# A decoder layer on one core: cross-attention with block-diagonal keys, and its stages as a pipeline over batches

## The chip, the cores and the metric

The kernel runs on one core of a Trainium2 chip. The metric is the time of one execution on the device, in microseconds (us); less is better. The engines named here are TensorE (PE, with its weight loads as PEld), VectorE (DVE), ScalarE (ACT), GpSimd (POOL) and SyncE (SP), which only issues transfers.

## The reference

For 4 batches of 512 tokens of width 256 (16 heads of 16), and a context of 64 rows a batch:

```
x = layernorm(x + attn(x) @ wo.T)
q2 = x @ wq + bq;  k2 = ctx @ wk + bk;  v2 = ctx @ wv + bv        # 16 heads, 64 keys
x = layernorm(x + softmax(q2 k2^T / 4) v2 @ xwo + bo)
probs = softmax(x @ router_w.T);  two largest of 8 experts a token
x = layernorm(x + sum_e w_e * gelu(x @ w1[e].T) @ w2[e].T)
```

Everything is float32. The two choices of expert make the logits' precision matter, so the kernel keeps scores at about float32's precision even where it uses narrower operands.

## The kernel before, in words

Each engine has its own list of instructions, in the order in which the program writes them; semaphores tie the lists together. There is no planner: the order is written out by hand.

**Self-attention** runs in 16 units (batch x four heads), `unit(u)`. A unit has 16 score tiles (128 keys x 512 queries), an exponential for each on ScalarE (L807), and four groups of `pv` (L1397), which multiply the values in and carry a column of ones for the sum. Row maxima run two units ahead, so the last two units (14 and 15) have none; they carry `context_v` and `context_k` instead, the projections of the context. The result, transposed, lies in `oT`.

**Ends.** `end_of_attention(ph, b, others)` finishes a batch; `ph` is 0 behind self-attention, 1 behind cross-attention. Each of its 4 tiles of 128 tokens passes through `turn_o` (L1455, four transposes), a reciprocal and a product on VectorE (L1055, L1057), `turn_back` (L1465, two transposes), a copy on ScalarE (L828), `out_proj` (L1473), and `add_residual` on VectorE (L1065, L1067, L1069). Once four tiles have their variance GpSimd raises it to the power -1/2 (L680), and VectorE writes the normalised rows (L1079). Each of these steps has two PSUM banks in turn. `turn_x` (L1485) transposes the rows again, ScalarE copies them (L832).

**Cross-attention, operands.** `q2_proj` (L1505) gives q2 transposed. q2 and k2 are cut into three bfloat16 parts (ScalarE L847 and L851, VectorE L1101, GpSimd L685), stored to DRAM and loaded back as a *stack*: 96 rows for each head, the six products of parts that matter one above another. A score is then one bfloat16 matmul of 96 rows. SyncE does these stores and loads (L498 to L514) and puts the maxima, also in three parts, into three more rows by small transfers (L391).

**Cross-attention, work.** `max2_tile` (L1523) makes the scores of 128 queries for 16 heads, 16 matmuls of 64 columns, and VectorE reduces 1024 columns (L1114). `max2_turn` and `max2_T` turn the maxima. `exp2_tile` (L1539) makes one head's scores, 64 keys x 512 queries with its maximum subtracted, and ScalarE takes the exponential (L882): 16 a batch, on 64 partitions. `pv2` (L1546) does four heads at once; VectorE copies the result to `oT` (L1139). The maxima of batch b+2 are made within batch b.

**Order around the change.** The ends of self-attention of all four batches come first, with turn and projection of the batch before them in between; then the cross-attention of four batches; then the ends of cross-attention with the routing of the batch two before them. Routing is about 21 small steps on VectorE (L1189 to L1228), two small groups on TensorE (`logits` L1615, `positions` L1624), and 8 indirect transfers a batch on GpSimd (L728). When all 32 have landed and the plan of tiles is made (L1260 on), tile metadata is loaded, rows are gathered, and 39 tiles go through their experts (L1658, L1669). Expert weights `wexp` are loaded by SyncE, one expert a cross-attention batch and five behind it (L520).

## Time and profile before

| what | value |
|---|---|
| median of 3 runs | 835.06 us (833.75 to 840.89) |
| the profiled execution | 832.12 us, its span 829.9 us |
| TensorE busy | 690.3 us, 83% of the span |
| VectorE busy | 353.1 us, 43% |
| ScalarE busy | 284.1 us, 34% |
| GpSimd busy | 219.3 us, 26% |
| mean granted TensorE clock | 0.909 of full |

Busy time is from the first to the last cycle of an instruction. Matmuls are pipelined: four in a row that are printed as one line last as long as four pitches and one latency. The idle time in brackets behind a row is that just before it on its engine, with what ended it. Self-attention ends at 269.2 us with the copy of its last unit, cross-attention's last unit at 423 us, the last rows before routing are normalised at 476.4 us, the first expert matmul is at 518.3 us, and the last at 806 us.

### The profile page before, as it was taken

The numbers are of one execution on the slowest core, as the hardware profiler recorded it, in microseconds if no ns is written. First come the engines' busy times: TensorE is split into PE (matmuls) and PEld (weight loads), VectorE is DVE, ScalarE is ACT, GpSimd is POOL, SyncE is SP. The second block draws the span as 40 slices with busy tenths as digits, with TensorE's granted clock in tenths as the row PEclk, the third lists the DMA queues.
The fourth block names the chain that finished last, engine by engine and source line by source line (L and its number), as shares of the span: only waits on it lengthen the run. The fifth ranks groups of instructions, "written<-read, shape, count | busy, mean of one in ns | idle before, by whom it ended". The sixth has DMA issues, their size and how long they took to land.

```text
span 829.9 us, 11914 instructions
## 1 busy us (share of the span) xinstructions
PE 690.3 (83%) x4099; PEld 444.7 (54%) x4100; DVE 353.1 (43%) x766; ACT 284.1 (34%) x513; POOL 219.3 (26%) x275
## 2 busy tenths in 40 slices
PE   6899999999998865757778520999999999999970
PEld 3322233322222644422147420899999999999960
DVE  3687877788972666643358750000000000000004
ACT  2246656667775233324632110111111111111112
POOL 2211111110120223210201672233333333333322
PEclk9869999999999989677899855999999999999995
DMA  5974133325343268592337233466666656666506
GB/s 158 190 166 82 15 80 75 78 70 105 58 138 89 21 104 124 95 139 55 99 111 249 52 54 111 137 177 180 181 184 178 176 159 178 178 179 183 169 11 203
DMA packets 69544, 103.60 MB, mean 125 GB/s; under 512 B 15556, under 2 KB 54909, under 8 KB 67966
## 3 DMA queue, kind: packets, MB, share of 16 engines
q1 hardware_dynamic: 56766, 90.44, 43.3%
q0 software_dynamic: 8512, 8.44, 6.2%
q10 hardware_dynamic: 4224, 4.19, 1.8%
q8 instruction: 22, 0.36, 0.2%
q14 instruction: 20, 0.16, 0.1%
HBM read 82.95 MB, written 21.40 MB: 126 GB/s over the span
## 4 chain that ended last, share of the span: by engine, by line
PE 69%; DVE 11%; DMA 7%; ACT 3%; POOL 3%; issue 3%; SPq 2%; DVEq 0%; POOLq 0%; ACTq 0%
PE ps L1658 17%; PE ps L1669 16%; PE ps L1397 7%; PE ps L1388 7%; PE ps L1322 6%; DVE nmx L966 3%; POOL metas L728 3%; PE ps L1473 3%; PE ps L1340 2%; PE ps L1546 2%; PE ps L1539 2%; ACT probs L807 2%; PE ps L1505 2%; DVE xr L1079 2%; DMA qst<-scr_q 1%
## 5 line engine op out<-in xcount | busy, mean ns | idle before, releaser
L807 ACT ACTIVATE probs<-ps 128x512 f32<-128x512 f32 x256 | 135.5, 603 | 92.0 <-PE ps L1388 91.3
L966 DVE TENSOR_REDUCE nmx<-ps 128x1 f32<-128x512 f32 x256 | 159.7, 679 | 15.7 <-PE ps L1322 15.2
L1658 PEld LDWEIGHTS ps<-xtT,w1c 128*128 128x128 f32 x1248 | 147.3, 194 | 4.3 <-issue 2.4
L1658 PE MATMUL ps<-xtT,w1c 128*128 128x128 f32 x1248 | 147.7, 277 | 1.8 <-ACT xtT L919 1.8
L1284 DVE TENSOR_SCALAR yw<-ps,mt 128x256 f32<-128x256 f32 x39 | 18.9, 484 | 292.0 <-PE ps L1669 292.0
L1669 PE MATMUL ps<-wexp,hidT 128*128 x624 | 141.0, 379 | 0.0
L1669 PEld LDWEIGHTS ps<-wexp,hidT 128*128 128x128 f32 x624 | 115.6, 190 | 14.1
L925 ACT ACTIVATE hidT<-ps 128x1024 f32<-128x1024 f32 x39 | 39.9, 1024 | 230.0 <-PE ps L1658 230.0
L767 POOL DMA_INDIRECT acc<-yw,mt x39 | 61.7, 1583 | 172.0 <-DVE yw L1284 172.0
L1322 PE MATMUL ps<-kst,qst 96*128 96x512 bf16 x256 | 99.2, 409 | 4.6 <-DVE nmx L966 3.3
L1388 PE MATMUL ps<-qst,kst 99*128 99x512 bf16 x256 | 93.4, 390 | 1.6 <-ACT probs L807 1.2
L1397 PE MATMUL ps<-probs,vu 128*32 128x512 f32 x512 | 68.2, 605 | 1.9 <-ACT probs L807 1.4
L1388 PEld LDWEIGHTS ps<-qst,kst 99*128 99x128 bf16 x256 | 23.6, 98 | 84.5 <-ACT probs L807 57.1
L882 ACT ACTIVATE probs<-ps 64x512 f32<-64x512 f32 x64 | 35.4, 587 | 41.5 <-PE ps L1539 41.4
L1322 PEld LDWEIGHTS ps<-kst,qst 96*128 96x128 bf16 x256 | 25.4, 99 | 44.4 <-DVE nmx L966 23.9
L759 POOL DMA_INDIRECT xt<-x2d,mt x39 | 40.8, 1046 | 31.5 <-DMA mt<-metas 12.0
L1539 PE MATMUL ps<-qst,k2st 99*64 99x512 bf16 x64 | 27.0, 468 | 13.9 <-DMA qst<-mT 8.5
L1647 PE MATMUL ps<-identf,xt 128*128 128x128 f32 x78 | 15.2, 277 | 27.9 <-DMA xt<-x2d,mt 27.9
L728 POOL DMA_INDIRECT metas<-meta,slot x32 | 31.6, 988 | 22.4 <-DVE slot L1226 13.9
L596 POOL TENSOR_TENSOR m<-nmx,one 128x16 bf16<-128x16 f32 x16 | 3.5, 217 | 126.5 <-DVE nmx L966 126.5
L1485 PE MATMUL ps<-identf,xr 128*128 128x128 f32 x64 | 13.7, 353 | 22.4 <-DVE xr L1079 21.6
L680 POOL TENSOR_TENSOR rstd<-ve,halves 128x4 f32<-128x4 f32 x8 | 10.9, 1364 | 72.0 <-DVE ve L1072 71.9
(177 smaller groups left out, 673.9 us busy)
## 6 DMA issues: line engine op xcount, KB each, us to landing
w1c<-in_w1T SPq DMA_DIRECT2D x39, 1024.0 KB, 5.4
wexp<-in_w2T SPq DMA_DIRECT2D x8, 1024.0 KB, 5.6
kst<-scrk SPq DMA_DIRECT2D x48, 128.0 KB, 7.0
qst<-scr_q SPq DMA_DIRECT2D x24, 256.0 KB, 9.1
qst<-scrq SPq DMA_DIRECT2D x8, 384.0 KB, 4.7
scr_q<-parts SPq DMA_DIRECT2D x4, 768.0 KB, 4.3
xTb<-in_xT SPq DMA_DIRECT2D x4, 512.0 KB, 8.4
qst<-scrq SPq DMA_DIRECT2D x8, 256.0 KB, 5.4
```

The source lines that it names most:

```text
L728: pool.indirect_dma_start(metas, bass.IndirectOffsetOnAxis(slot[b % 2][:, k * QT + t:k * QT + t + 1], 0), meta[k][:, 2 * (QT * b + t):2 * ...
L759: pool.indirect_dma_start(xt[t % 2][:, :], None, x2d, bass.IndirectOffsetOnAxis(slot_meta(t, 0).bitcast(U32), 0), **checked()).then_inc(s_ ...
L767: pool.indirect_dma_start(acc, bass.IndirectOffsetOnAxis(slot_meta(t, 0).bitcast(U32), 0), yw[t % 2][:, :], None, **checked(), compute_op= ...
L807: act.activation(probs[n % 8][:, :], ps[:, 4 + n % 3, :], ACT.Exp).then_inc(s_exp, 1)
L925: act.activation(hidT[j % 2][:, :], bank(2 * (j % 2), 2), ACT.Gelu).then_inc(s_h, 1)
L966: dve.tensor_reduce(nmx[w % 2][:, k:k + 1], ps[:, ring_bank("max", w, k), :], AX.X, ALU.max, negate=True).then_inc(s_mfree, 1)
L1322: pe.matmul(ps[:, ring_bank("max", w, k), :], qst[0:ROWS, q_cols(w, h) + qt * P:q_cols(w, h) + (qt + 1) * P], kst[0:ROWS, k_cols(w, h):k_c ...
L1388: pe.matmul(ps[:, 4 + n % 3, :], kst[:, k_cols(u, h) + kt * P:k_cols(u, h) + (kt + 1) * P], qst[:, q_cols(u, h):q_cols(u, h) + S], start=T ...
L1397: mm = pe.matmul(ps[VW * h:VW * (h + 1), 7, :], vu[u % 2][:, (kt * HG + h) * VW:(kt * HG + h + 1) * VW], probs[(kt % 2) * HG + h][:, :], s ...
L1539: pe.matmul(ps[0:SC, 4 + h % 2, :], k2st[0:MROWS, ds((h * NB + b) * SC, SC)], qst[0:MROWS, ds((b * H + h) * S, S)], start=True, stop=True) ...
L1658: mm = pe.matmul(ps[:, 2 * (j % 2) + f // 4, f % 4 * P:(f % 4 + 1) * P], w1c[j % 2][:, k * FF + f * P:k * FF + (f + 1) * P], xtT[j % 2][:, ...
L1669: mm = pe.matmul(ps[:, 4 + j % 2, 0:D], hidT[j % 2][:, f * P:(f + 1) * P], wexp[:, ds(e * EW + f * D, D)], start=(f == 0), stop=(f == KF - 1))
```

## The change

- **Keys in diagonal blocks.** `k2h[m]` and `k2l[m]` hold, for the 8 heads of half m and each batch, 64 columns per head in which only that head's 16 rows of k2 are not zero. They are made on chip from k2 and the mask `mine`: 128 x 2048 elements each, two by VectorE (`k2_high_blocks`), two by GpSimd (`k2_blocks`). k2 and q2 are each cut in two: a high part, which is the value cast to `float32r`, and a low part, value minus high part, `float32r` too. No part goes to DRAM; the stacks, their stores and loads, and GpSimd's `split_q2` are gone.
- **Scores.** `max2_tile(b, i)` is one bank of 512 columns (8 heads x 64 keys, 128 queries): three `float32r` matmuls of 512 columns, high x high, high x low, low x high; 8 a batch. `exp2_tile(b, p)` does two heads on 128 partitions: three such matmuls, and one bfloat16 matmul of `pick` with the turned maxima, which subtracts them; 8 a batch. Exponentials are 8 a batch on 128 partitions. `pv2` multiplies pairs of heads with the block-diagonal `v2bd`, two products a group. The copy of the result moves from VectorE to ScalarE. `context_v` is done twice, for partitions 0 to 63 and 64 to 127.
- **Order.** The end of batch 0's self-attention is put between the score tiles of unit 15. Then come seven stages. Stage n holds the end of self-attention of batch n (e1), cross-attention of batch n-1 (x), the end of cross-attention of batch n-2 (e2) and routing of batch n-3 (r), interleaved on each engine by hand. The ends have one bank for each step now; maxima, scores and q2 share banks 5 and 6 (`ring2`).
- **Transfers.** SyncE issues the stores of the normalised rows (ScalarE did). Experts 0, 1 and 7 are loaded once self-attention is done, 2 and 3 after the last cross-attention, then 4 and 5, and 6 after the last logits. GpSimd issues a batch's 8 scatters in one piece, behind the power of the stage before.

The diff, cut to its core:

```diff
+    def tiles_of(ph, b):
+        return QT * E_AT[ph, b]
+    def ring2(i):
+        return 6 - i % 2
...
-        def split_q2(b):
-            pool.wait_ge(s_q2c[2], b + 1)
...
+        def k2_blocks(out, part, m):        # GpSimd
+            pool.tensor_tensor(out[:, :].rearrange("p (b h k) -> p b h k", h=HB, k=SC),
+                               part[:, m * NB * SC:(m + 1) * NB * SC].rearrange("p (b k) -> p b k", k=SC).unsqueeze(2)
+                               .to_broadcast([P, NB, HB, SC]),
+                               mine[:, :].unsqueeze(1).unsqueeze(3).to_broadcast([P, NB, HB, SC]), ALU.mult).then_inc(s_k2l, 1)
+        for m in range(KD):
+            k2_blocks(k2l[m], k2tl, m)
...
+        for n in range(NB + 3):             # GpSimd
+            if n < NB:
+                rstd_of(0, n)
+                add_bias(n)
+            if 0 <= n - 2 < NB:
+                rstd_of(1, n - 2)
+            if n == NB + 2:
+                pool.wait_ge(s_on, NE_TILES)
+                for i in range(2):
+                    pool.memset(xt[i][:, :], 0.0).then_inc(s_xt0, 1)
+            if n >= 3:
+                scatter_metas(n - 3)
...
+            dve.tensor_copy(k2th[:, :], k2t[:, :]).then_inc(s_k2p, 1)
+            dve.tensor_tensor(k2tl[:, :], k2t[:, :], k2th[:, :], ALU.subtract).then_inc(s_k2p, 1)
...
+        def first_end():                    # VectorE, in unit 15
+            norm_o(0, 0, 0)
+            norm_o(0, 0, 1)
+            k2_high_blocks(0)
+            for t in range(2):
+                norm_o(0, 0, 2 + t)
+                add_residual(0, 0, t)
+            k2_high_blocks(1)
+            for t in range(2, QT):
+                add_residual(0, 0, t)
...
+        FIRST_END = {5: 0, 7: 1, 9: 2, 11: 3, 13: 4, 15: 5}   # TensorE, by score tile of unit 15
...
+        def max2_tile(b, i):
+            t, m = i // KD, i % KD
+            pe.wait_ge(s_ql, b + 1)
+            if i >= 2:
+                pe.wait_ge(s_m2f, NP * b + i - 1)
+            at, keys = m * S + t * P, slice(b * HB * SC, (b + 1) * HB * SC)
+            high, low = qh[b % 2][:, at:at + P], ql[b % 2][:, at:at + P]
+            pe.matmul(ps[:, ring2(i), :], high, k2h[m][:, keys], start=True, stop=False)
+            pe.matmul(ps[:, ring2(i), :], high, k2l[m][:, keys], start=False, stop=False)
+            pe.matmul(ps[:, ring2(i), :], low, k2h[m][:, keys], start=False, stop=True).then_inc(s_m2r, 1)
...
+        def exp2_tile(b, p):
+            pe.wait_ge(s_m2c, b + 1)
+            if p >= 2:
+                pe.wait_ge(s_exp2, NP * b + p - 1)
+            pe.matmul(ps[:, ring2(p), :], k2h[m][:, at:at + P], high, start=True, stop=False)
+            pe.matmul(ps[:, ring2(p), :], k2h[m][:, at:at + P], low, start=False, stop=False)
+            pe.matmul(ps[:, ring2(p), :], k2l[m][:, at:at + P], high, start=False, stop=False)
+            pe.matmul(ps[:, ring2(p), :], pick[:, p * P:(p + 1) * P], mT2[:, :], start=False, stop=True).then_inc(s_e2, 1)
...
+        def stage(n):                       # TensorE; "if" lines left out
+            turn_x(1, r, 0); turn_x(1, r, 1)
+            e1_step(0);  max2_tile(x, 0); max2_tile(x, 1)
+            e1_step(1);  max2_tile(x, 2); max2_tile(x, 3);  logits(r, range(QT))
+            e1_step(2);  max2_tile(x, 4); max2_tile(x, 5)
+            e1_step(3);  max2_tile(x, 6); max2_tile(x, 7)
+            e1_step(4);  e1_step(5);  e2_step(0);  max2_turn(x)
+            e2_step(1);  exp2_tile(x, 0); exp2_tile(x, 1)
+            e2_step(2);  exp2_tile(x, 2); exp2_tile(x, 3);  turn_x(0, e1, 0); turn_x(0, e1, 1);  pv2(x, 0)
+            e2_step(3);  positions(r);  exp2_tile(x, 4); exp2_tile(x, 5);  pv2(x, 1)
+            e2_step(4);  exp2_tile(x, 6); exp2_tile(x, 7);  pv2(x, 2);  q2_proj(e1, 0)
+            e2_step(5);  q2_proj(e1, 1);  pv2(x, 3)
...
+        def stage(n):                       # VectorE; "if" lines left out
+            norm_o(0, e1, 0);  row_max2(x, 0); row_max2(x, 1)
+            norm_o(0, e1, 1);  row_max2(x, 2); row_max2(x, 3)
+            norm_o(0, e1, 2);  add_residual(0, e1, 0);  row_max2(x, 4); row_max2(x, 5);  router_logits(r)
+            norm_o(0, e1, 3);  add_residual(0, e1, 1);  row_max2(x, 6); row_max2(x, 7);  max2_parts(x);  probabilities(r)
+            add_residual(0, e1, 2); add_residual(0, e1, 3);  norm_o(1, e2, 0);  max2_T(x)
+            normalise(0, e1);  choose(r, 0);  norm_o(1, e2, 1);  second_choice(r)
+            norm_o(1, e2, 2);  add_residual(1, e2, 0);  norm_o(1, e2, 3);  add_residual(1, e2, 1);  slots(r)
+            add_residual(1, e2, 2); add_residual(1, e2, 3);  q2_low(e1);  normalise(1, e2)
...
+        def turn_o(ph, b, t):
+            n = tiles_of(ph, b) + t
+            if n >= 1:
+                pe.wait_ge(s_on, n)
...
+            for i in range(2):              # context_v
+                for b in range(NB):
+                    for k in range(KD):
+                        mm = pe.matmul(ps[i * SC:(i + 1) * SC, b // 2, (b % 2) * D:(b % 2 + 1) * D],
```

On ScalarE a stage takes, in this order: the copies of `turn_x(1, r)`, four of e1's `o2` copies, the router's exponential, then the exponentials in pairs with e2's copies, the copies of `turn_x(0, e1)` and of cross-attention's result between them, and last `q2_out` (both halves), `q2_high`, and the last result copy.

## Rows read from the trace of the kernel before

**Rows 1.** The windows: engines' busy time (and instructions), granted clock, DMA share, GB/s, by stretch.
```profile
55.00:255.00 200.00, 195.85 (x1018) 60.39 (x1017) 154.04 (x263) 130.27 (x248) 31.11 (x91) 1.00 0.37 82
282.00:332.00 50.00, 34.52 (x170) 25.59 (x169) 31.80 (x74) 17.68 (x29) 12.13 (x6) 0.89 0.64 95
360.00:424.00 64.00, 47.30 (x305) 13.05 (x304) 26.66 (x35) 32.16 (x58) 8.72 (x6) 0.82 0.42 77
424.00:477.00 53.00, 39.39 (x246) 33.44 (x246) 41.46 (x153) 10.65 (x26) 17.78 (x18) 0.91 0.54 159
```
**Rows 2.** The chain of waits, 290 to 520 us: start, length, what.
```profile
346.09 12.36 DMA qst<-scr_q
369.00 8.41 DMA qst<-mT
```
**Rows 3.** Timeline, end of unit 15: start, length, engine, line, operation, count, idle before.
```profile
257.44 0.82 PE L1388 MATMUL ps<-qst,kst 99*128 99x512 bf16 x3
...
263.61 1.07 PE L1397 MATMUL ps<-probs,vu 128*32 128x512 f32 x8
...
266.01 1.06 PE L1397 MATMUL ps<-probs,vu 128*32 128x512 f32 x8
...
269.22 0.69 DVE L1045 COPY oT<-ps 128x512 f32<-128x512 f32 x1 [5.29 <-PE ps L1397]
```
**Rows 4.** Timeline, TensorE's pieces of the ends, the q2 projection and the logits.
```profile
285.01 1.88 PE L1505 MATMUL ps<-xTs,xwq_s 128*128 128x512 f32 x4
...
431.37 1.04 PE L1455 MATMUL ps<-identf,oT 128*128 128x128 f32 x8
...
437.46 0.60 PE L1455 MATMUL ps<-identf,oT 128*128 128x128 f32 x4
...
438.11 1.03 PE L1473 MATMUL ps<-xwo_s,o 128*128 128x256 f32 x4
...
440.12 0.95 PE L1615 MATMUL ps<-rw_s,xTs 128*128 128x8 f32 x8
```
**Rows 5.** Groups by line and form on VectorE, 268 to 490 us: busy, mean ns.
```profile
L1114 DVE TENSOR_REDUCE nmx<-ps 128x16 f32<-128x1024 f32 x16 | 19.4, 1222 | 17.7 <-PE ps L1523 17.6
...
L1067 DVE BATCH_NORM_STATS2 bst<-ybuf 128x6 f32<-128x256 f32 x32 | 13.7, 428 | 1.1
L1057 DVE TENSOR_TENSOR osb<-ps,rec 128x256 f32<-128x256 f32 x32 | 13.6, 424 | 1.1
L1065 DVE TENSOR_TENSOR ybuf<-ps,xr 128x256 f32<-128x256 f32 x32 | 13.5, 421 | 16.8 <-PE ps L1473 16.7
L1055 DVE RECIPROCAL rec<-ps 128x16 f32<-128x16 f32 x32 | 7.9, 245 | 6.6 <-PE ps L1455 6.4
...
L1101 DVE TENSOR_TENSOR q2t<-q2t,parts 128x1024 f32<-128x1024 f32 x4 | 4.9, 1220 | 3.3 <-ACT parts L847 3.3
```
**Rows 6.** The same groups on ScalarE.
```profile
L832 ACT ACTIVATE xTs<-ps 128x512 f32<-128x512 f32 x16 | 9.6, 598 | 33.4 <-PE ps L1485 33.4
L841 ACT ACTIVATE q2t<-ps,bq_s 128x512 f32<-128x512 f32 x8 | 5.5, 688 | 17.2 <-PE ps L1505 17.2
L847 ACT ACTIVATE parts<-q2t 128x1024 bf16<-128x1024 f32 x4 | 4.2, 1058 | 0.1
```
**Rows 7.** The same groups on GpSimd.
```profile
L680 POOL TENSOR_TENSOR rstd<-ve,halves 128x4 f32<-128x4 f32 x8 | 10.9, 1364 | 72.0 <-DVE ve L1072 71.9
...
L711 POOL TENSOR_TENSOR xr<-xr,bo_s 128x1024 f32 x3 | 7.0, 2337 | 0.0
```
**Rows 8.** The tile `xr` on VectorE: shortest, median and longest duration in ns.
```profile
L1079 DVE TENSOR_SCALAR xr<-ybuf,mv,rstd x32: 395/408/2275, 280.2 to 476.0; 128x256 f32<-128x256 f32 x32
```
**Rows 9.** Timeline, the last normalised rows, the last slots and the last scatter.
```profile
474.83 1.53 DVE L1079 TENSOR_SCALAR xr<-ybuf,mv,rstd 128x256 f32<-128x256 f32 x4 [1.89 <-POOL rstd L680]
...
488.44 0.22 DVE L1226 TENSOR_REDUCE slot<-prod 128x8 uint32<-128x64 f32 x1
...
500.28 0.95 POOL L728 DMA_INDIRECT metas<-meta,slot  x1 [0.31 <-issue]
```

More of the change, by code:

```diff
@@ L80, in ring_order @@
     return order + [("turn", NUN - 1)]
+NP = H // 2
+MAXW = 3 * H
+E_ORDER = ((0, 0), (0, 1), (0, 2), (1, 0), (0, 3), (1, 1), (1, 2), (1, 3))
+E_AT = {part: n for n, part in enumerate(E_ORDER)}
+NE_TILES = 2 * NT
 RING = {use: n for n, use in enumerate(ring_order())}
@@ L589, in _, with copy @@
         pool.wait_ge(s_m3, 2)
-        def copy(to, of):
-            v = one[0:of.shape[0], :]
+        def copy(to, of, start=0):
+            v = one[start:start + of.shape[0], :]
             for _ in of.shape[2:]:
@@ L914, in _ @@
+        for n in range(NB + 3):
+            stage(n)
         act.activation(ahead[:, 2:3], ahead[:, 1:2], ACT.Gelu)
@@ L1247, in _ @@
+        for n in range(NB + 3):
+            stage(n)
         planned = [0]
@@ L1507, in q2_proj @@
             mm.then_inc(s_q2, 1)
-        pe.wait_ge(s_v2, 1)
-        pe.wait_ge(s_k2c[0], 2)
-        def turn_x_q(b, pair):
-            if pair == 0:
-                pe.wait_ge(s_q2t, 2 * b)
-            turn_x(0, b, pair)
-        def max2_tile(b, t):
-            if not (isinstance(b, int) and b == 0 and t < 2):
-                pe.wait_ge(s_m2f, QT * b + t - 1)
-            slot = 2 * (t % 2)
-            for h in range(H):
-                mm = pe.matmul(ps[:, slot + h // 8, (h % 8) * SC:(h % 8 + 1) * SC],
-                               qst[0:ROWS, ds((b * H + h) * S + t * P, P)],
-                               k2st[0:ROWS, ds((h * NB + b) * SC, SC)], start=True, stop=True)
-            mm.then_inc(s_m2r, 1)
@@ L1633, in _, with stage, e1_step, e2_step @@
-        for b in range(NB + 1):
-            end_of_attention(1, b, {} if b == 0 else {
-                1: lambda: turn_x(1, b - 1, 0), 2: lambda: turn_x(1, b - 1, 1), 3: lambda: positions(b - 2) if b >= 2 else None,
-                4: lambda: logits(b - 1, (0, 1)), 5: lambda: logits(b - 1, (2, 3))})
-        positions(NB - 1)
+        pe.wait_ge(s_k2h, KD)
+        pe.wait_ge(s_k2l, KD)
+        pe.wait_ge(s_v2bd, 2)
+        def stage(n):
+            e1, x, e2, r = (n - k if 0 <= n - k < NB else None for k in range(4))
+            def e1_step(step):
+                if e1 is not None and n > 0:
+                    end_step(0, e1, step)
+            def e2_step(step):
+                if e2 is not None:
+                    end_step(1, e2, step)
+            if r is not None:
+                turn_x(1, r, 0)
+                turn_x(1, r, 1)
+            e1_step(0)
+            if x is not None:
+                max2_tile(x, 0)
+                max2_tile(x, 1)
+            e1_step(1)
+            if x is not None:
+                max2_tile(x, 2)
+                max2_tile(x, 3)
+            if r is not None:
+                logits(r, range(QT))
+            e1_step(2)
+            if x is not None:
+                max2_tile(x, 4)
+                max2_tile(x, 5)
+            e1_step(3)
+            if x is not None:
+                max2_tile(x, 6)
+                max2_tile(x, 7)
+            e1_step(4)
+            e1_step(5)
+            e2_step(0)
+            if x is not None:
+                max2_turn(x)
+            e2_step(1)
+            if x is not None:
+                exp2_tile(x, 0)
+                exp2_tile(x, 1)
+            e2_step(2)
+            if x is not None:
+                exp2_tile(x, 2)
+                exp2_tile(x, 3)
+            if e1 is not None:
+                turn_x(0, e1, 0)
+                turn_x(0, e1, 1)
+            if x is not None:
+                pv2(x, 0)
+            e2_step(3)
+            if r is not None:
+                positions(r)
+            if x is not None:
+                exp2_tile(x, 4)
+                exp2_tile(x, 5)
+                pv2(x, 1)
+            e2_step(4)
+            if x is not None:
+                exp2_tile(x, 6)
+                exp2_tile(x, 7)
+                pv2(x, 2)
+            if e1 is not None:
+                q2_proj(e1, 0)
+            e2_step(5)
+            if e1 is not None:
+                q2_proj(e1, 1)
+            if x is not None:
+                pv2(x, 3)
@@ L1638, in _ @@
+        for n in range(NB + 3):
+            stage(n)
         pe.wait_ge(s_rt, RT * NB)
-        pe.matmul(ps[:, 7, 128:128 + NE], onesb[:, :], base[:, :], start=True, stop=True).then_inc(s_cnt, 1)
+        pe.matmul(ps[:, RB, RC + 128:RC + 128 + NE], onesb[:, :], base[:, :], start=True, stop=True).then_inc(s_cnt, 1)
         def turn_tile(t, j, turn):
```

821 lines of the change are left out of this document (378 added, 443 removed).

## The prediction, made before the changed kernel was run

> **What bounds the kernel now.** I read the windows first, stretch by stretch. In self-attention TensorE is busy 196 of 200 us at the full clock [rows 1]: nothing of that stage is touched. From 269 to 477 us it is not so: the ends of self-attention keep TensorE busy 69% of the time, cross-attention 74% at a granted clock of 0.82, the last ends 74% at 0.91 [rows 1]. No engine is full; waits are the bound. The chain of waits names two long ones, 12.4 and 8.4 us, both transfers into the stack [rows 2]; the rest is short handovers at batch ends. The expert stage behind has no part in the change. So I sum the stretch from unit 15 to the last scatter of metadata, which starts at 500.28 [rows 9]: the expert stage waits for that transfer, the plan and the load of metadata, all unchanged.
>
> **Prices on TensorE.** Eight float32 transposes take 1.04 and four 0.60, so one costs 0.11 and the rest is latency; an output projection is four instructions of about 0.217, 0.87; a q2 projection half is 1.7 (1.88 with its latency), both 3.4; sixteen logits instructions are 1.7 (eight take 0.95) [rows 4]. The end of a batch is 16 + 8 transposes and 4 projections: 2.7 + 3.5 = 6.2, and 0.9 for `turn_x`. A bfloat16 matmul of 512 columns has a pitch of 0.215: three end after 0.82, latency included; a group of values takes 1.07, about 0.86 as pitch [rows 3].
>
> **The price that no row shows** is that of a `float32r` matmul of 512 columns. The nearest rows are bfloat16 at 0.215 [rows 3] and float32, two instructions of 0.43, 0.86 together [rows 4]. Nothing excludes a gain, but I know no row below 0.215, so the bounds are 0.215 and 0.86. I take 0.215: the diff forms value minus cast value as a low part, and that would be zero if the type kept all of float32; a narrower operand is nearer to the bfloat16 row.
>
> The Trainium skill (FP8 and Floating Point Precision, TensorE Precision Notes) says that true float32 needs four passes through the array and that a reduced form cuts the 4-byte value to about 22 bits; one pass each would be the 0.215 of my sum, and no trace here shows it.
>
> A batch of cross-attention then costs TensorE 24 x 0.215 = 5.2 for maxima, 32 x 0.215 = 6.9 for scores, 4 x 0.86 = 3.4 for values, 0.4 for turning: 15.9. That is more than now (the maxima were 64 columns each, the scores one product): what goes is waiting, not work.
>
> **Part 1, units 14 and 15.** `context_v` twice is 16 more instructions of 0.217, 3.5, of which idle slots hide 0.5: +3. The end of batch 0 adds 6.2 to unit 15, where four tiles take 2.4 now [rows 3] and TensorE needs 4 x 0.215 + 0.86 = 1.7 of that; the slots hide 2, waits for reciprocals and copies add about 2.7: +6.9. The variance of batch 0 would stand at 269.1 + 3 + 6.9 = 279.0. Now the mask products. On VectorE one is twice the 1.22 of a 1024-element subtraction, 2.4 [rows 5]; on GpSimd twice 2.34, 4.7 [rows 7]. One of four normalised rows takes 2.28 instead of 0.41 when GpSimd reads SBUF beside it [rows 8]: the two engines block each other for a whole instruction. GpSimd's run 266 to 270.7; VectorE's first would start at 267.7, is held to 270.7 and ends at 273.1; GpSimd's second then runs to 277.6 or so, VectorE's second to 280; two residual sums are behind it in the queue, and TensorE's last projection waits for the first of them. That is 3.3 late: the variance stands at 282.3.
>
> The Trainium skill (SBUF — State Buffer, two separate sides) states the same as a rule: the port pair that VectorE and GpSimd share is locked for the whole instruction. Without it the sum would be 3.3 less.
>
> **Part 2, stage 0.** Nothing covers this chain: power 1.4 [rows 7], first two rows 0.8, turn 0.45, copy 0.7 [rows 6], turn 0.5, copy 0.8, both projections 3.4, bias copy 0.9, high part 1.1 [rows 6], low part 1.3 [rows 5], handovers 0.6. 282.3 + 12.0 = 294.3, when maxima can start.
>
> **Part 3, stage 1** (end of batch 1, cross-attention of 0). Maxima and end steps: TensorE 5.2 + 6.2 = 11.4. VectorE, per 512-column maximum 0.65 (half of 1222 ns and some fixed cost), per tile of the end 0.67 + 1.1 [rows 5], 13.2 with the splits. In queue order each waits for the other by 0.2 to 0.4 at a pair; TensorE ends its last projection at +13.3, the turn of the maxima waits behind it, its copy waits behind the residual sum: +15.7. Then scores, values, turn, q2: 6.9 + 3.4 + 0.9 + 3.4 = 14.6, the last value group beside other work (-0.9), 1.2 + 0.3 for `turn_x`'s copy queued behind two exponentials, and the bias copy, high and low parts at the end, 3.4: 18.5. Together 34.2. ScalarE has 8 exponentials of 0.6, four result copies and the rest, 15 of 34: not a bound.
>
> **Stage 2** adds the end of cross-attention, 6.2 of TensorE work that VectorE's 7 overlap: 40.3. **Stage 3** adds routing: `turn_x` waits for rows normalised behind `q2_low` (+3.2), logits 1.5, the second reciprocal queued behind `choose` 1.5, positions 0.6: 47.1. **Stage 4** has no end of self-attention: maxima at the pace of two banks, (0.65 + 0.65 + 0.33)/2 = 0.82 each, 6.6, with logits, splits and copy 11.8; scores, values and end 15.6, `turn_x` at the start 3.0, rounding and the router's small steps 0.5: 30.9. Sum of the four 152.5, for 119.5 of TensorE work (26.4, 32.6, 35.5, 25.0), 78%.
>
> **Stage 5** is VectorE's: variance 1.5, power and rows 2.1, turns and copies 2.6, logits 1.9, the end and the routing in one queue 13.1, power 1.3: 22.5. The last rows are normalised from 294.3 + 152.5 + 22.5 = 469.3, against 474.83 [rows 9]: 5.5 earlier.
>
> **Part 4, the tail.** The last slots come 13.6 after that row, as now [rows 9]: 482.9. Now GpSimd is behind by then, with 8 older scatters of 0.95 + 0.31 in its queue; after the change those of batch 2 are finished at 480, behind the power, and cover nothing. Batch 3's start at 483.4, the last of them 7 x 1.26 later, 492.2 against 500.28: 8.1 saved.
>
> **What is moved past queues.** SyncE's stores of rows come before two expert loads each; the last store is queued behind loads 4 and 5, 2 MB issued a stage earlier, done by then. Expert 6 is loaded after the last logits, about 478, and lands before the plan at 488. Without that cover its landing would delay the first expert matmul. ScalarE loses eight issues, nothing gained. GpSimd's bias (2.3 a batch) can hold one of VectorE's small steps, within the 0.5 above. The title speaks of rows normalised on VectorE; they are already (L1079), so this part does nothing.
>
> **Sum.** 832.1 - 8.1 = 824.0 for the profiled execution. The median of the runs shown is 2.9 above it, so **827**.
>
> **Rivals.**
> - *Float32r is slower (other side).* Place: the 192 such matmuls, in stages 1 to 4, where TensorE leads. At two passes, 0.43, it is 192 x 0.215 = 41 more: 868; at float32's 0.86, 124 more: 951. It decides from a pitch of 0.215 + 16.4/192 = 0.30, where the time passes 843.4. For it: no row of the type. Against: the low part above. 0.10.
> - *The lower clock.* The stages are full of handovers, as cross-attention is now, with 0.82 granted. 119.5 us of work at 0.82 is 145.7: +26, 853. For: four waits of 1 to 3 us in each stage, and the 8 us of stage 0. Against: TensorE is 78% busy there, and got 0.91 at 74% [rows 1]. 0.19.
> - *The interleaving is better than I queue it.* At the 98% of self-attention [rows 1] the four stages would take 122, 30 less: 797; halfway, 812. For: now that VectorE, ScalarE and TensorE each have other work in a stage, waits may overlap which I added. Against: one bank a step in the ends, two for scores, and in-order queues. 0.24.
> - My own case, 0.45; something else, 0.02.
>
> **Numbers.** A measurement of this kernel tells about 1% from no change, 826.7 to 843.4. My case lies on its edge: errors of 8 us a side put 0.23 below and 0.22 within. The better interleaving gives 0.24 below. The clock gives 0.05 within and 0.14 above, float32r 0.10 above, the rest 0.02 above. Faster 0.47, same 0.27, slower 0.26. The range 798 to 862 leaves out float32r at two passes or more (0.10) and the ends of two others (0.08).
>
> **What would show it.** Float32r: the pitch of `exp2_tile`'s matmuls. Part 1: VectorE's block products lengthened beside GpSimd's, and the variance of batch 0 near 282. Stage lengths: the first score tiles of the four batches about 40 us apart, and the granted clock over 0.9 from 294 to 447. Tail: scatters of batch 3 starting at 483. I would be wrong if a queue holds a whole stage, above all `q2_low` with the normalised rows behind it, or if the clock falls in stage 0 and stays down.

## The result, and the profile after

The changed kernel took **845.95 us** (median of 5 runs, 844.56 to 854.81), the kernel before 837.24 beside it: a ratio of **1.013, 95% interval 1.008 to 1.018**. I had forecast 827, faster. It is slower by 1.3%. The profiled execution, 854.81 us, is the slowest of its five, and one of the experiments ran the same kernel again: 847.21, profiled 848.

The page after. TensorE is busy 42 us longer than before (690.3 there; how much of that is work and how much a lower clock, a busy time doesn't tell), the transfers are 11 MB fewer, and the chain of waits has moved from transfers (7% to 4%) to TensorE (69% to 74%):

```profile
PE 732.6 (86%) x3963; PEld 473.5 (56%) x3964; DVE 340.0 (40%) x766; ACT 272.1 (32%) x493; POOL 218.7 (26%) x270
...
PEclk9879999999999886998899665699999999999995
...
DMA packets 58907, 92.79 MB, mean 109 GB/s; under 512 B 13841, under 2 KB 45298, under 8 KB 57331
...
PE 74%; DVE 10%; DMA 4%; ACT 4%; issue 3%; POOL 2%; SPq 1%; POOLq 0%; DVEq 0%; ACTq 0%
```

Windows cut at the variance of batch 0, at the first maxima tile of batches 0 to 3, and at the start of stage 5 (columns as in [rows 1]):

```profile
55.00:255.00 200.00, 195.84 (x1018) 61.32 (x1018) 152.75 (x261) 129.25 (x246) 37.24 (x100) 1.00 0.39 83
282.70:297.90 15.20, 8.41 (x21) 3.99 (x21) 3.47 (x8) 3.62 (x5) 3.39 (x2) 0.78 0.64 208
297.90:342.70 44.80, 39.78 (x132) 20.73 (x132) 15.51 (x40) 12.21 (x21) 3.37 (x2) 0.77 0.00 1
342.70:388.60 45.90, 38.94 (x180) 24.88 (x181) 23.73 (x64) 14.44 (x27) 4.40 (x3) 0.97 0.04 13
388.60:440.10 51.50, 44.05 (x198) 28.61 (x197) 27.73 (x86) 14.29 (x28) 8.10 (x7) 0.89 0.04 12
440.10:471.40 31.30, 28.86 (x136) 18.08 (x135) 16.17 (x52) 8.61 (x17) 4.74 (x5) 0.95 0.20 32
471.40:500.00 28.60, 18.21 (x77) 13.95 (x77) 14.87 (x55) 3.55 (x8) 11.09 (x11) 0.67 0.87 184
```

Self-attention is as it was. TensorE is busy 85 to 92% of the four stages, where I had 78%, and in two stretches the granted clock is 0.77 to 0.78: there its two levels, 0.5 and 1.00 of full, alternate.

Stage by stage, in us. A stage starts with the first maxima tile of its batch, stage 5 with the last product with the values of batch 3. The last column is a second execution of the same kernel (the first experiment), at 848.36 us closer to the median:

| stretch | forecast | trace after | second execution |
|---|---|---|---|
| variance of batch 0 at | 282.3 | 282.7 | 284.9 |
| stage 0, to the first maxima | 12.0 | 15.2 | 13.6 |
| stage 1 | 34.2 | 44.9 | 37.9 |
| stages 2 to 4 | 118.3 | 128.7 | 130.3 |
| stage 5, to the last rows | 22.5 | 27.2 | 25.8 |
| last rows to last scatter | 22.9 | 22.6 | 22.6 |
| last scatter starts at | 492.2 | 521.2 | 515.2 |

**The score tile.** The timeline of TensorE in stage 2, at the full clock, and under it the weight loads of the same tile:

```profile
358.44 0.48 PE L1566 MATMUL ps<-qh,k2h 128*128 128x512 f32 x1
358.76 0.40 PE L1567 MATMUL ps<-ql,k2h 128*128 128x512 f32 x1
358.99 0.40 PE L1568 MATMUL ps<-qh,k2l 128*128 128x512 f32 x1
359.32 0.39 PE L1569 MATMUL ps<-mT,pick 48*128 48x512 bf16 x1
359.64 0.50 PE L1566 MATMUL ps<-qh,k2h 128*128 128x512 f32 x1
```

```profile
358.76 0.19 PEld L1568 LDWEIGHTS ps<-qh,k2l 128*128 128x128 f32 x1
359.32 0.09 PEld L1569 LDWEIGHTS ps<-mT,pick 48*128 48x128 bf16 x1 [0.37 <-issue]
359.64 0.19 PEld L1566 LDWEIGHTS ps<-qh,k2h 128*128 128x128 f32 x1 [0.23 <-issue]
```

From tile to tile it is 1.20 (358.44 to 359.64), not the 0.86 of my sum. One step, 358.76 to 358.99, is 0.23: a float32r matmul costs about what a bfloat16 one does, as I took it. The other three steps are 0.32 to 0.33. Tiles come in pairs, and a whole pair takes 2.40 to 2.51 at the full clock, not 1.72. The weights of the 48-row matmul, and the next ones, are loaded only when their matmul starts, while the others are loaded one matmul ahead.

**Batch 0's end.** Block products on VectorE and on GpSimd (each in a window of its own), the variance, TensorE's waits for ScalarE's copies in unit 15, and the first wait of stage 0:

```profile
267.75 3.53 DVE L1049 TENSOR_TENSOR k2h<-k2th,mine 128x2048 fp32r<-128x2048 f32 x1
...
275.91 2.26 DVE L1049 TENSOR_TENSOR k2h<-k2th,mine 128x2048 fp32r<-128x2048 f32 x1
...
282.69 0.17 DVE L1091 TENSOR_SCALAR ve<-mv 128x4 f32<-128x4 f32 x1
```

```profile
265.52 3.62 POOL L713 TENSOR_TENSOR k2l<-k2tl,mine 128x2048 fp32r<-128x2048 f32 x1 [5.73 <-DVE k2tl L1044]
...
269.10 5.67 POOL L713 TENSOR_TENSOR k2l<-k2tl,mine 128x2048 fp32r<-128x2048 f32 x1
```

```profile
268.84 0.41 PE L1446 MATMUL ps<-identf,osb 128*128 128x128 f32 x2 [1.33 <-ACT o L814]
...
273.14 0.41 PE L1446 MATMUL ps<-identf,osb 128*128 128x128 f32 x2 [1.05 <-ACT o L814]
...
276.61 0.41 PE L1446 MATMUL ps<-identf,osb 128*128 128x128 f32 x2 [1.33 <-ACT o L814]
...
285.18 0.52 PE L1530 MATMUL ps<-identf,xr 128*128 128x128 f32 x3 [2.66 <-DVE xr L1098]
```

**The tail**, against [rows 9]: last normalised rows, last slots, last scatter. Rows to slots 13.1 where it was 13.6; slots to scatter 9.4.

```profile
498.61 1.41 DVE L1098 TENSOR_SCALAR xr<-ybuf,mv,rstd 128x256 f32<-128x256 f32 x4 [1.16 <-POOL rstd L724]
...
511.75 0.22 DVE L1206 TENSOR_REDUCE slot<-prod 128x8 uint32<-128x64 f32 x1
...
521.17 0.96 POOL L735 DMA_INDIRECT metas<-meta,slot  x1 [0.30 <-issue]
```

### The profile page after: what moved, and what is told of

Same layout as the page of the kernel before. It is cut to its first block, busy times and chain, and to the rows that moved or that the text cites. A ratio compares the mean times of both kernels' runs of the same rounds, so it can differ in the third digit from the quotient of the medians.

```text
span 852.8 us, 11545 instructions
## 1 busy us (share of the span) xinstructions
PE 732.6 (86%) x3963; PEld 473.5 (56%) x3964; DVE 340.0 (40%) x766; ACT 272.1 (32%) x493; POOL 218.7 (26%) x270
## 4 chain that ended last, share of the span: by engine, by line
PE 74%; DVE 10%; DMA 4%; ACT 4%; issue 3%; POOL 2%; SPq 1%; POOLq 0%; DVEq 0%; ACTq 0%
PE ps L1699 17%; PE ps L1710 15%; PE ps L1426 7%; PE ps L1417 7%; PE ps L1351 6%; PE ps L1455 3%; DVE nmx L983 3%; PE ps L1369 2%; PE ps L1538 2%; ACT probs L823 2%; POOL metas L735 2%; PE ps L1566 2%; PE ps L1576 2%; PE ps L1438 1%; PE ps L1569 1%
## 5 line engine op out<-in xcount | busy, mean ns | idle before, releaser
L823 ACT ACTIVATE probs<-ps 128x512 f32<-128x512 f32 x256 | 136.0, 604 | 102.8 <-PE ps L1417 102.1
L983 DVE TENSOR_REDUCE nmx<-ps 128x1 f32<-128x512 f32 x256 | 159.8, 680 | 15.7 <-PE ps L1351 15.2
L1351 PEld LDWEIGHTS ps<-kst,qst 96*128 96x128 bf16 x256 | 25.5, 99 | 44.5 <-DVE nmx L983 23.9
L724 POOL TENSOR_TENSOR rstd<-ve,halves 128x4 f32<-128x4 f32 x8 | 8.2, 1026 | 152.3 <-DVE ve L1091 152.3
L1688 PE MATMUL ps<-identf,xt 128*128 128x128 f32 x78 | 15.2, 277 | 26.9 <-DMA xt<-x2d,mt 26.9
L867 ACT ACTIVATE probs<-ps 128x512 f32<-128x512 f32 x32 | 19.1, 597 | 44.0 <-PE ps L1569 44.0
L814 ACT ACTIVATE o<-ps 128x256 f32<-128x256 f32 x32 | 12.2, 382 | 56.3 <-PE ps L1446 56.3
```

Source lines behind the costliest of these rows:

```text
L823: act.activation(probs[n % 8][:, :], ps[:, 4 + n % 3, :], ACT.Exp).then_inc(s_exp, 1)
L983: dve.tensor_reduce(nmx[w % 2][:, k:k + 1], ps[:, ring_bank("max", w, k), :], AX.X, ALU.max, negate=True).then_inc(s_mfree, 1)
L1351: pe.matmul(ps[:, ring_bank("max", w, k), :], qst[0:ROWS, q_cols(w, h) + qt * P:q_cols(w, h) + (qt + 1) * P], kst[0:ROWS, k_cols(w, h):k_c ...
```

## The experiments

All were timed beside the kernel before, in five series (its median in them: 837.14, 835.82, 836.19, 837.61, 836.18). R is the ratio to it, with its 95% interval. Between series R is the fairer measure: a difference of two medians and the same difference by R can be 1 to 3 us apart. The theory after the result: the score tiles are dearer than forecast, and a lower clock takes the rest. The rival: the waits between queues set the pace, whatever TensorE has to do.

### The changed kernel again; the 48-row matmuls side by side; extra matmuls in two stages; one product

> The changed kernel as it is, again. Theory A (switches of operand type on TensorE): in every profile a score tile of exp2_tile takes 1.20 us at the full clock instead of 0.86. Theory B (the lower clock): the profiled execution, 9 us above the median of its own kernel, lost them to stretches at half clock in stages 0 and 1; with a shorter span those stretches are shorter and nothing else is. Both: 843 to 848 us.

847.21 us, R 1.011 [1.007, 1.015]. In this execution stage 1 ran at the full clock, 36.3 us from variance to variance; in the first profile it ran at 0.77 and took 44.9, and that one was the longer.

```diff
-  high*k2h, high*k2l', low*k2h, pick*mT2            (every tile)
+  products, pick*mT2 | pick*mT2, products           (odd tiles begin with the 48-row one)
```

> In tiles with odd p the bfloat16 matmul with the maxima comes first instead of last, so that two of four changes between float32r and bfloat16 in a pair of tiles go. Theory A: 16 pairs save about 0.3 us each, 4 to 6 us less than the changed kernel. Theory B, and the theory that waits and not TensorE's work set the stages: no difference over 1 us.

848.16, R 1.010 [1.006, 1.014]. Pairs of tiles took 2.21 to 2.41 instead of 2.40 to 2.51: 0.1 to 0.2 less, where theory A had 0.3. By time there is no gain, as theory B had it, but 2 to 3 us would not show in this interval: not settled by this run.

```diff
+  def filler(count): count x matmul(ps[:, RB, :], pick[:, 0:P], pick[:, 0:S])
+  stage 0: filler(11), (4), (3) around turn_x;  stage 1: filler(11), (5), (5) ahead of its waits
```

> Idle time of TensorE in stages 0 and 1 is filled with bfloat16 matmuls of 512 columns into an unused bank (11 before the first turn_x, 4 and 3 in stage 0, 11 before the first maxima, 5 and 5 before the scores of batch 0). Theory B: the granted clock stays at its upper level there, both q2 projections take 3.4 instead of 6.3 us and the scores of batch 0 lose 7: up to 10 less than the changed kernel in an execution like the profiled one, 3 to 6 in the median. Rival: the clock falls elsewhere anyway, and the filler delays what waits: 0 to 3 more.

844.06, R 1.010 [1.007, 1.012]: 3 us by the medians, 1 by R, so by time no gain is shown. The profile shows one: variance to variance over stage 0 fell from 29.4 to 26.2 us, at a clock of 1.00 instead of 0.88, and stage 0 itself took the 12.0 of my sum. The clock still fell later, to 0.69 in stage 5.

```diff
-  matmul(high, k2h); matmul(high, k2l); matmul(low, k2h)
+  matmul(high, k2h)                                  (maxima and scores)
```

> Scores from high x high alone: the two products with a low part are left out in maxima and scores (128 of 192 float32r matmuls; the output is less precise). Theory that TensorE's work leads the stages: 128 x 0.23 = 29 us less than the changed kernel, at least 22. Rival, that handovers lead them: under 12 less.

846.68, R 1.010 [1.006, 1.014]: **29 us of TensorE's work out, nothing gained**, which the rival expected (under 12). The windows from the variance of batch 0 to 500 us, first of the changed kernel (second profile), then of this one:

```profile
284.90:500.00 215.10, 174.66 (x757) 111.52 (x758) 101.43 (x303) 57.91 (x107) 39.67 (x34) 0.88 0.23 54
```

```profile
282.70:500.00 217.30, 173.82 (x631) 102.17 (x631) 99.88 (x304) 58.36 (x107) 40.03 (x35) 0.75 0.23 54
```

126 matmuls fewer in the trace (the edit leaves out 128), the same busy time: the granted clock fell from 0.88 to 0.75. A busy share alone can't tell less work at a low clock from more at a high one; the count and the clock beside it do. TensorE's waits of over 0.15 us added up to 41 and 43 us in these windows, so this could still have been the rival.

### The clock held up by extra matmuls in all stages

```diff
+  filler(bank, count) ahead of TensorE's waits over 0.6 us, in a bank that is free there:
+  stage starts (bank 2), between turn_x pairs (2, 7), before the last projection (0),
+  before max2_turn and e2_step(1) (7), before positions (7)
```

> The changed kernel with extra bf16 matmuls (512 columns, 3 to 12 at a place) put ahead of every wait of TensorE over 0.6 us in stages 0 to 6, in banks that are free there; nothing of the computation changes. With fillers in stages 0 and 1 alone the granted clock after the variance of batch 0 was 1.00 until about 370 us and then 0.88, 0.92, 0.92, 0.65, and the time 844.1. If idle stretches of TensorE bring the clock down, it is over 0.95 in all stages now, and the last variance comes 8 to 12 us sooner: 832 to 838. If the clock has another cause, or what is filled is not what the stages wait for, 843 to 847.

**839.43**, R 1.004 [1.002, 1.006]: between the two branches.

> Leaves out both low products of the maxima and of the scores (128 float32r matmuls, 29 us of TensorE's work at full clock), as the run with one product did, and has the same extra matmuls ahead of TensorE's waits as the run before this one in the job. Theory 1 (the removed work was given back by the clock alone, 0.75 instead of 0.88): the clock is over 0.9 and the time falls to 815 to 825. Theory 2 (the stages are bound by chains of waits between TensorE, VectorE and ScalarE, whose length doesn't depend on TensorE's work): the clock is over 0.9 too, TensorE's idle time grows, and the time stays within 5 us of the run with one product, 841 to 848. Between 825 and 841: both take a share, which the idle time in the profile divides.

**831.24**, R 0.994 [0.991, 0.998]. Both windows:

```profile
282.50:500.00 217.50, 206.87 (x939) 118.40 (x937) 107.43 (x333) 59.73 (x110) 44.41 (x41) 0.94 0.24 59
```

```profile
286.50:500.00 213.50, 190.12 (x811) 100.58 (x809) 108.29 (x340) 59.94 (x110) 50.13 (x46) 0.87 0.25 61
```

With the fillers TensorE did useless work and the kernel got 7.8 us faster than the changed one (5 us by R, 0.6%); what the edit leaves of the computation is the same, and what changed beside the fillers is the clock, 0.88 to 0.94. With the fillers in, leaving out the products brings 8.2 us, where it brought 0.5 without. So a lower clock had taken back part of the removed work in the run before. The 8 are not 29, though. The stages tell why. In stages 1 and 2 both filled runs had the full clock, and the 7.4 us of products left out of each brought 4.7 and 5.0: waits took the rest. In stage 4 the clock fell from 1.00 to 0.74, and nothing came of it. Both theories hold a part.

```diff
+  matmul(low, k2l)                                   (maxima and scores: a fourth product)
```

> The changed kernel with a fourth float32r product (low half times low half) in each of the 32 maxima tiles and 32 score tiles: 64 more matmuls, 14.7 us of TensorE's work at full clock. If work and clock trade against each other (as when 29 us of work were left out and the time stayed), the clock rises to over 0.93 after the variance of batch 0, and the time grows by 0 to 7 us: 846 to 854. If TensorE's work leads at a given clock, 860 to 863. If waits lead, under 5 us more at an unchanged clock.

859.08, R 1.029 [1.025, 1.032]: 11.9 more by the medians, 15 by R, for 14.7 of work, at 0.92. That is closest to the second branch. Added work is paid nearly or wholly in full; the trade of work against clock that I expected here gave back 3 at most.

### The waits: copies sooner, rows first

```diff
-  FIRST_O2 = {9: 0, 11: 1, 13: 2, 15: 3}
+  FIRST_O2 = {7: 0, 9: 1, 11: 2, 13: 3}
```

> The changed kernel with ScalarE's four copies of batch 0's turned heads queued one exponential pair sooner in unit 15 (behind exponentials 7, 9, 11, 13 in place of 9, 11, 13, 15). TensorE waits 1.33, 1.05, 1.33 and 0.96 us for them now. If those waits are on the path, the variance of batch 0 comes 2.5 to 4 us sooner (279 to 280.5 instead of 282.7) and the time is 842 to 844; if the exponentials themselves set the pace of unit 15, the copies only move the wait, and the variance stays at 282 to 283.

842.68, R 1.008 [1.005, 1.012]. The variance stood at 283.11, but this execution also reached unit 15's end work later. From its first turn (267.58) to the variance is 15.53; in both profiles of the changed kernel it is 18.43 (264.26 to 282.69). So 2.9 us sooner, as the first branch had it; it is 15.53 or 15.54 in all four later versions with this edit too. By time alone (4.5 us by the medians, 2 by R) the intervals overlap.

```diff
-  q2_low(e1); normalise(1, e2)        (VectorE, end of a stage)
+  normalise(1, e2); q2_low(e1)
```

> The changed kernel with VectorE's last two pieces of a stage exchanged: the rows of the batch two back are normalised ahead of the low half of q2. TensorE waits 2.76, 2.76, 2.29 and 3.3 us at the starts of stages 3 to 6 for those rows. If these waits are on the path, each gets 0.7 to 1 us shorter (the subtraction for the low half takes that long), the low half comes later where nobody waits for it yet, and the time is 843 to 845. If TensorE's work and clock set the pace, or the low half is late in its place, 846 to 848.

**840.63**, R 1.005 [1.003, 1.008]: 6.6 us by the medians, 5 by R, more than the 2 to 4 expected. The waits at the starts of stages 5 and 6 stayed (2.29 and 3.30). Those of stages 3 and 4 fell by 2.2, not by 0.7 to 1: from 2.76 to

```profile
376.42 0.66 PE L1530 MATMUL ps<-identf,xr 128*128 128x128 f32 x4 [0.55 <-DVE xr L1098]
```

and from the variance before that start to the next it was 21.3 us at a clock of 1.00, where the second execution of the changed kernel had 26.5 at 0.83. The wait was 2.2 shorter and the stretch 5.2: in these two profiles a wait went with a lower clock behind it. I had counted only the length of the low half. The second execution of the changed kernel shows that it also stood waiting for ScalarE's high half, with the rows behind it:

```profile
377.24 1.23 DVE L1118 TENSOR_TENSOR ql<-q2t,qh 128x1024 fp32r<-128x1024 f32 x1 [2.21 <-ACT qh L861]
```

### What the score tile costs

```diff
-  k2h, k2l, k2th, k2tl, qh, ql = F32R
+  k2h, k2l, k2th, k2tl, qh, ql = BF16
```

> The changed kernel with both halves of k2 and of q2 kept as bf16 instead of float32r: the same three products, so the same number of matmuls, but a score tile has no change of operand type in it. The three low-order parts are coarser than before, which changes the computation a little. My theory of the missed term (0.23 a float32r matmul and 0.1 us at each change of type) expects a score tile of 0.86 to 0.90 us instead of 1.20 and a maxima tile of 0.65 instead of 0.69, together 11 us of TensorE's work less; the rival (1.20 comes from the waits of the tile, not from its types) expects 1.1 to 1.2 still. On the time: if less work is given back by the clock, as with one product, 844 to 848; if not, 834 to 838.

841.27, R 1.005 [1.002, 1.007]. The time lies between the branches. The tile, with one record missing, took 1.07 (361.00 to 362.07), so **my theory of the change of type falls**: the steps at the 48-row matmul are still 0.31 and 0.32. Only the first step, 0.32 before, is 0.22.

```profile
361.00 0.38 PE L1566 MATMUL ps<-qh,k2h 128*128 128x512 bf16 x1
361.22 0.38 PE L1567 MATMUL ps<-ql,k2h 128*128 128x512 bf16 x1
361.75 0.39 PE L1569 MATMUL ps<-mT,pick 48*128 48x512 bf16 x1
362.07 0.39 PE L1566 MATMUL ps<-qh,k2h 128*128 128x512 bf16 x1
```

```diff
+  the bf16 halves and the fillers of all stages together
```

> The bf16 blocks of the run before this one in the job together with extra matmuls ahead of TensorE's waits in all stages. With fillers, leaving out 29 us of work brought 8.2 us (839.4 to 831.2), 0.28 of it. If that ratio holds, 11 us less bring 3 us: 835 to 838. If work counts fully once the clock is held, 827 to 831.

833.86, R 0.996 [0.993, 0.998]: 5.6 us less than the float32r version with fillers (7 by R), between the two branches.

```diff
+  these two, FIRST_O2 = {7: 0, 9: 1, 11: 2, 13: 3}, and normalise(1, e2) ahead of q2_low(e1)
```

> A version to beat both kernels: bf16 blocks, extra matmuls ahead of the waits, ScalarE's copies of batch 0 one pair of exponentials sooner, rows normalised ahead of the low half of q2. The copies alone brought 4.5 us (847.2 to 842.7), though the variance of batch 0 came no sooner in the profile (283.1); if the parts add up, 829 to 834. If they are the same microseconds, 835 to 838, no better than the run before this one in the job.

828.99, R 0.989 [0.987, 0.992]: the parts add up, and it is the first version about 1% faster than the kernel before.

```diff
-  mT2 = sb("mT2", S, BF16, R_P, MAXW);  pick = sb("pick", NP * P, BF16, Y_REG, MAXW)
+  mT2 = sb("mT2", S, BF16, R_P);        pick = sb("pick", NP * P, BF16, Y_REG)
+  dve.memset(mT2[:, :], 0.0)            (once, stage 1; pick's rows past 48 are zero by its own selects)
```

> The changed kernel with the picking matrix and the turned maxima zero-padded from 48 to 128 rows, so that the bf16 matmul of a score tile has as many rows as the three float32r ones. With bf16 blocks a score tile still took 1.07 us in steps of 0.22, 0.22, 0.31, 0.32: what is left over 0.88 lies ahead of the 48-row matmul and behind it. If the change of the number of rows is its price, a tile of the changed kernel falls from 1.20 to about 1.00, and TensorE's work by 32 x 0.2 = 6.4 us; if the change of operand type or of accumulation is, it stays at 1.20. The time, by the share that came back when work was left out without fillers (9 and 0 us of 11 and 29), 841 to 847.

841.07, R 1.006 [1.003, 1.009], at the lower end of the expectation. Float32r and bf16 in one tile as in the changed kernel, all with 128 rows, from 359.58 to 360.51 in stage 2:

```profile
359.58 0.58 PE L1571 MATMUL ps<-qh,k2h 128*128 128x512 f32 x1
360.00 0.40 PE L1572 MATMUL ps<-ql,k2h 128*128 128x512 f32 x1
360.24 0.39 PE L1573 MATMUL ps<-qh,k2l 128*128 128x512 f32 x1
360.47 0.39 PE L1574 MATMUL ps<-mT,pick 128*128 128x512 bf16 x1
360.51 0.58 PE L1571 MATMUL ps<-qh,k2h 128*128 128x512 f32 x1
360.93 0.39 PE L1572 MATMUL ps<-ql,k2h 128*128 128x512 f32 x1
```

```profile
360.47 0.10 PEld L1574 LDWEIGHTS ps<-mT,pick 128*128 128x128 bf16 x1 [0.27 <-issue]
360.47 0.20 PEld L1571 LDWEIGHTS ps<-qh,k2h 128*128 128x128 f32 x1
```

**0.93 a tile.** (The first record of a tile begins early: 0.04 behind the one before and 0.42 ahead of the next are two steps of 0.23.) So 0.27 of this tile's missing 0.34 was the 48-row matmul among 128-row ones. A whole pair takes 1.93 to 2.13 instead of 2.40 to 2.51, 0.2 or a little more a tile, and stages 2 to 4 fell from 130.3 to 123.4 us. More rows made it faster. The padded weights are still loaded only as their matmul starts; what is new is that the next ones are loaded beside them, one matmul ahead.

```diff
+  the combined bf16 version with the padding
```

> The combined version (bf16 blocks, extra matmuls, sooner copies, rows first; 829.0) with the padding of the run before this one in the job. If the padding takes 0.2 us off a tile, 823 to 827; if it doesn't, 828 to 830.

825.03, R 0.984 [0.980, 0.988]: as the first branch had it.

### Is the clock the change's own loss, and what is left when all is mended

```diff
+  filler(...) in the kernel before: ahead of turn_x (10), turn_back at a batch start (8, 3),
+  the maxima of batch 2 (30), cross_batch 0 and 1 (7, 20)
```

> The kernel before the change with extra matmuls ahead of TensorE's longest waits of 280 to 477 us (the rows of x normalised on ScalarE, the stacks and maxima rows that come by DMA), nothing of the computation changed. Its clock was 0.89, 0.62, 0.82 and 0.91 in the four stretches. If its waits are on DMAs and on other engines, a higher clock there buys less than in the changed kernel (7.8 us): 832 to 836. If the clock costs it as much, 826 to 830, and then the change and its combined version have gained nothing by themselves that the same filling would not have brought without it.

831.43, R 0.991 [0.988, 0.995], between the two branches. So the kernel before loses to the clock too, by 5 to 10 us as far as these fillers show. They aren't the best ones: in the profile, at 837.34 slower than the median, the clock still fell to 0.73 over 360 to 424. A fair comparison of the mended versions is with this one.

```diff
+  padding, fillers, sooner copies, rows first; qh, ql, k2h, k2l stay F32R
```

> The changed kernel with its own float32r halves kept, and the four edits together: padding to 128 rows, extra matmuls ahead of the waits, sooner copies, rows first. With bf16 halves these four gave 825.0. With the padding in, a float32r matmul follows the others at 0.23 us, bf16 at 0.22, so only 5 x 32 x 0.01 = 2 us of TensorE's work separate the two: 825 to 829. If bf16 brings more than that (smaller writes on VectorE and ScalarE, quicker weight loads), 830 to 834.

**820.81**, R **0.981 [0.977, 0.984]**: faster than either branch, and than the bf16 version, which I had not expected. Against the kernel before with its fillers (0.991) the change, mended, is about 1% faster, and the intervals are apart. Its window:

```profile
279.70:500.00 220.30, 187.77 (x939) 114.18 (x937) 110.14 (x341) 59.50 (x110) 50.52 (x46) 0.95 0.26 63
```

```diff
-  the fillers of that version
```

> The run before this one in the job without the extra matmuls. Alone, against 847.2, padding brought 6.1 us, rows first 6.6, copies 4.5: if they add up without fillers 830; if a part of them is given back by a lower clock where TensorE has less to do, 833 to 838, and the granted clock over 282 to 470 us is under 0.92.

827.51, R 0.989 [0.985, 0.993]: faster than both branches had it, at a clock of 0.93 over 282 to 470. So of the 3.0% between the changed kernel and the mended one, 2.2 are the padding and the two orders, 0.9 the fillers. Singly, padding gave 0.5, rows first 0.6, copies 0.3 and fillers 0.6, in sum 2.0. That the four help one another is likely from this, but not shown: each of the four differences holds the error of the changed kernel's own R, 0.4%.

## Why the prediction was wrong, step by step

**The steps that failed.** In the profile the last scatter came 29 us later than forecast (521.2 against 492.2), in the second execution 23. The stretch behind it, which I held unchanged, took 331.6 us instead of 329.6; it was 329.7 to 332.4 in all versions of the changed kernel.

1. *"32 x 0.215 = 6.9 for scores".* The term counted four equal matmuls a tile. Measured 1.20 a tile, 0.34 more, or 2.40 to 2.51 a pair: 11 to 13 us over 32 tiles at the full clock. For stages 2 to 4 that is 8 to 9.5 us, and the 72 float32r matmuls of their maxima at 0.23 instead of 0.215 add 1.1. The sum has the size of their 10.4, but that isn't a proof: a clock of 0.89 to 0.97 and shorter waits than I had are in the 10.4 too. The rival "float32r is slower" watched the wrong number: its pitch, 0.23, was never near the 0.30 from which it decides. The row that was missing is a 48-row matmul among 128-row ones, and [rows 3] shows 99-row ones next to each other. The padded run settles it in the trace: 0.93 a tile, and 6.9 us less in stages 2 to 4. By time it is weaker, R 0.5% lower: the sizes of both intervals, 0.3 to 0.4% to a side, are of the order of that gain.

2. *"Against: TensorE is 78% busy there, and got 0.91 at 74%".* I gave the lower clock 0.19 and let my own case, whose prices are all of the full clock, have none of it. It was in the result. In the first profile stage 0 took 3.2 more than forecast (the q2 projections 6.3 instead of 3.4), and stage 1 was 7 us longer than in the second execution, at 0.77 against 0.96. From that second execution to the one with all fillers the way from the variance to the last scatter fell by 6 us, of the 23. Stage 5 took 4.7 and 3.3 more than forecast, at 0.68 and 0.71; in the mended version, at the full clock, it took 22.3, my 22.5. The extra matmuls gave 7.8 us back (5 by R); with one product and no fillers next to nothing of 29 came through. In rows 1 the ordering of busy share and clock is not even monotonic (0.89 at 69%, 0.82 at 74%), and I read it as a rule. What the traces show is finer: the clock was low behind stretches with waits of 1 to 3 us, and 0.98 to 1.00 in stages 0 to 4 once their waits were filled. They don't give a whole account either. Stage 5 stayed at 0.75 with its waits filled, TensorE busy 25.5 of 27.4 us, and with one product stage 4 ran at 0.74 in spite of its fillers; no run shows why.

With the tile padded and the clock held up the sum of the stages comes out: stages 0 to 5 of the mended version took 186.3 us, forecast 187.0. Part of that is luck, as its order of rows also takes out waits that I had counted.

**Forecast, and there.** *"`turn_x` waits for rows normalised behind `q2_low` (+3.2)"* was 2.76, and *"waits for reciprocals and copies add about 2.7"* was 4.7 for the four copies. They are no part of the miss beyond those 2 us. What I overlooked is that they are not the change's nature: exchanging two lines on VectorE, and one number a copy on ScalarE, brought 5 to 6.6 and 2 to 4.5 us.

**Right by the wrong part.** The variance of batch 0 at 282.3 came at 282.7, and that is in part luck: in other executions of the same code up to there it came as late as 286.5, as self-attention ended later. The lock that I took from [rows 8] is there. VectorE's block product starts at 267.75 beside GpSimd's first, which ends at 269.14, and takes 3.53 instead of 2.26: 1.39 of GpSimd's were left, and VectorE lost 1.27. GpSimd's second, begun at 269.10, takes 5.67 instead of 3.62: 2.19 of VectorE's were left, and GpSimd lost 2.05. It is so in all executions of the changed kernel. The Trainium skill (SBUF — State Buffer, two separate sides) has the shared port locked for the whole instruction; both delays agree with it to 0.15 us. Wrong were GpSimd's price, 3.62 and not 4.7, so that VectorE's product ended at 271.3 and not at 273.1 and its second, begun at 275.91, met nothing; and the path. TensorE's last projection waited for ScalarE's copy (0.96), not for the residual sum, and the other three waits of the four turns are for copies too. So the 3.3 for the lock fell away, and the copies' 4.7 instead of 2.7 filled 2 us of its place; the rest I can't divide. The Trainium skill's other rule (FP8 and Floating Point Precision, TensorE Precision Notes) has four passes for true float32. The trace agrees: 0.86 for 512 columns in float32 [rows 4], and about a quarter, 0.23, in float32r.

**Right.** Self-attention. The tail: 22.6 after the last rows, forecast 22.9, with batch 2's scatters done by then as forecast. The interleaving (rival, 0.24) was better than I queued it: TensorE was idle 2 to 7 us a stage, 22 in the four, where my sum had 33. The dearer work and the lower clock took that up, and more; without this gain the miss would have been larger.

**The chance.** Slower by over 1% had 0.26; the range to 862 held 846. The case that came true was a mixture of two rivals' mechanisms, a dearer tile and a lower clock, that I had set apart as exclusive, each with a size of its own.

## What to carry to other kernels

A matmul with fewer rows between ones with 128 can cost more than its columns, as the 48-row one did here: look at the step from start to start across it, and pad it with zeros if that step is longer. Read TensorE's busy time only beside the number of matmuls and the granted clock: work removed from a stage full of short waits may come back as a lower clock, so remove or fill the waits first, then the work. When an engine's queue has one piece that someone waits for and one that nobody does, put the awaited one first: here that shortened two waits by 2.2 us each, where the other piece is 1.2 us long and had waited itself.

## What the runs showed of the hardware

- Useless matmuls ahead of waits made the changed kernel faster: 839.4 against 847.2, granted clock 0.94 against 0.88 after the first variance.
- 128 matmuls fewer left TensorE's busy time where it was (173.8 and 174.7 us), at 0.75 instead of 0.88.
- A 48-row bf16 matmul of 512 columns between 128-row ones takes 0.32 and makes the next start 0.32 later; the next weights are loaded only as their matmul starts. With 128 rows it fits in steps of 0.23, float32r before and behind it, so the change of operand type costs nothing by itself. Why the rows matter, the trace doesn't say.
- VectorE's and GpSimd's products with two operands in SBUF, begun beside each other, held each other up until the earlier one ended: 3.53 instead of 2.26 us, and 5.67 instead of 3.62.
- With bf16 halves the mended kernel took 825.0, with float32r 820.8, ratios 0.984 [0.980, 0.988] and 0.981 [0.977, 0.984]. The intervals overlap. In the profiles the bf16 version is 1.7 us quicker from the variance to the end of stage 4, as its cheaper matmuls would have it, and loses 5.4 behind it: stage 5 takes 26.1 at a clock of 0.93 where the float32r one takes 22.3 at 1.00. Why the clock differs there stays open.
